# Attention with ALiBi and one key-value head: the fp32 matmuls of a step in two groups instead of three, the maxima's transpose moved

## The reference, cut to what matters

```python
q = (hidden_states @ Wq).reshape(b, s, NUM_HEADS, HEAD_DIM)
kv = hidden_states @ Wkv
k, v = (kv[..., :HEAD_DIM], kv[..., HEAD_DIM:])
scores = jnp.einsum('bqhd,bkd->bhqk', q, k) * scale
bias = slopes[:, None, None] * (pos[None, None, :] - pos[None, :, None]).astype(jnp.float32)
scores = jnp.where(causal[None, None], scores + bias[None], -jnp.inf)
attn = jax.nn.softmax(scores, axis=-1)
out = jnp.einsum('bhqk,bkd->bqhd', attn, v).reshape(b, s, h)
return out @ Wo
```

## Time and profile before

| | us |
|---|---|
| median of 3 runs | 821.62 |
| lowest and highest | 820.59, 821.73 |
| the profiled execution's own time | 822.31 |
| its span, first to last instruction | 820.5 |
| PE busy | 806.4 |
| DVE busy | 594.7 |
| POOL busy | 429.4 |
| ACT busy | 372.5 |

### The profile page before, as it was taken

The page is one execution under the profiler, slowest core; times in us unless marked ns, Lnnn a source line. Parts: engine busy times, 40 slices in busy tenths (PEclk is TensorE's granted clock), DMA queues, the critical chain, the costliest instruction groups (busy, mean ns, idle before and its releaser), DMA issues.

```text
span 820.5 us, 13647 instructions
## 1 busy us (share of the span) xinstructions
PE 806.4 (98%) x4618; PEld 583.2 (71%) x4618; DVE 594.7 (72%) x1589; ACT 372.5 (45%) x730; POOL 429.4 (52%) x313
## 2 busy tenths in 40 slices
PE   7999999999999999999999999999999999999997
PEld 5777878888665655556555555688887888888886
DVE  3877554577878889988888896255647779684877
ACT  1755536232466677676666665221401231051322
POOL 1000000000299998899889988522746298363566
PEclk9999999999999999999999999999999999999999
DMA  8867687467566655676566655462064613500012
GB/s 313 315 199 209 229 256 256 154 177 223 152 140 150 152 132 146 146 160 143 134 146 172 156 122 172 151 180 89 1 224 136 198 60 111 194 28 1 38 65 103
DMA packets 71390, 125.85 MB, mean 153 GB/s; under 512 B 7460, under 2 KB 16708, under 8 KB 71240
## 3 DMA queue, kind: packets, MB, share of 16 engines
q1 hardware_dynamic: 71312, 124.97, 52.5%
q10 hardware_dynamic: 8, 0.01, 0.0%
HBM read 85.61 MB, written 38.94 MB: 152 GB/s over the span
## 4 chain that ended last, share of the span: by engine, by line
PE 77%; DMA 7%; DVE 6%; issue 4%; ACT 4%; POOL 1%; SPq 0%; DVEq 0%; POOLq 0%; ACTq 0%
PE p_s L870 11%; PE p_st L899 9%; PE p_o L910 9%; PE p_s L978 5%; PE p_s L980 5%; PE p_s L979 5%; PE p_o L923 5%; PE p_o L809 4%; DMA inv_b<-inv_d 3%; PE p_s L809 2%; PE p_st L978 2%; PE p_st L980 2%; PE p_st L979 2%; PE p_s L1003 2%; PE p_s L1002 2%
## 5 line engine op out<-in xcount | busy, mean ns | idle before, releaser
L1452 DVE CUSTOM_DVE_ANT_0 spill<-p_s,mask 128x128 bf16<-128x128 f32 (+3 forms) x512 | 219.6, 483 | 38.3 <-PE p_s L870 37.6
L1169 ACT ACTIVATE pt<-p_st 128x512 f32<-128x512 f32 (+1 forms) x352 | 178.2, 562 | 101.1 <-PE p_st L899 100.9
L635 POOL TENSOR_SCALAR_AFFINE_SELECT pt<-pt 128x512 f32<-128x512 f32 x128 | 87.5, 696 | 238.7 <-ACT pt L1169 238.7
L870 PE MATMUL p_s<-kst,xt 98*128 98x128 f32 (+3 forms) x512 | 151.1, 343 | 0.9 <-DVE mx L1452 0.7
L899 PE MATMUL p_st<-xt,kst 100*128 100x512 f32 (+1 forms) x352 | 129.4, 387 | 0.7 <-DMA xt<-ml 0.3
L870 PEld LDWEIGHTS p_s<-kst,xt 98*128 98x128 f32 x512 | 91.4, 189 | 52.7 <-DVE mx L1452 42.7
L642 POOL TENSOR_TENSOR pt<-pt 128x1536 f32<-128x1536 f32 x32 | 111.8, 3492 | 2.7
L910 PE MATMUL p_o<-pt,vst 128*32 128x512 f32 (+3 forms) x1024 | 82.4, 439 | 0.0
L648 POOL TENSOR_TENSOR pt<-pt 128x1024 f32<-128x1024 f32 x32 | 76.7, 2396 | 0.0
L899 PEld LDWEIGHTS p_st<-xt,kst 100*128 100x128 f32 x352 | 64.5, 190 | 14.1 <-issue 5.6
L809 PE MATMUL p_o<-xt,wqh 128*128 128x512 f32 x136 | 53.1, 400 | 0.8 <-DVE xt L1603 0.8
(11 more groups left out here) (205 smaller groups left out, 1648.0 us busy)
## 6 DMA issues: line engine op xcount, KB each, us to landing
xt<-qh_d SPq DMA_DIRECT2D x64, 256.0 KB
xs<-in_x_t_dram SPq DMA_DIRECT2D x32, 256.0 KB, 6.2
qh_d<-qh SPq DMA_DIRECT2D x32, 256.0 KB, 3.2
ql_d<-ql SPq DMA_DIRECT2D x32, 256.0 KB, 4.1
xt<-ql_d SPq DMA_DIRECT2D x32, 256.0 KB
o_d<-o_st SPq DMA_DIRECT2D x32, 256.0 KB, 2.3
ob<-o_d SPq DMA_DIRECT2D x32, 256.0 KB, 5.5
xin<-in_x_dram SPq DMA_DIRECT2D x14, 512.0 KB, 7.8
```

The lines of the kernel that those rows point to most:

```text
L635: pool.affine_select(out=own, in_=own, compare_op=ALU.is_ge, fill=0.0, base=0, pattern=[[0, 4], [1, P]], channel_multiplier=-1).then_inc(c ...
L870: pe.matmul(scores_of(n), qst[s % 4][0:R_MAX, j, qb * P:(qb + 1) * P], kst[0:R_MAX, b * S:b * S + keys], start=True, stop=True).then_inc(s ...
L1169: act.activation(pt[s % 2][:, j:j + heads, PT_AT[kb]:PT_AT[kb] + KB_LEN[kb]], p_st[:, place(k) % 3, 0:heads * KB_LEN[kb]].rearrange("p (j ...
L1452: dve.tensor_tensor_reduce(spill[:, SPILL_AT[qb]:SPILL_AT[qb] + keys], scores_of(n), mask[:, S - keys:S], 1.0, LOWEST, ALU.add, ALU.max, m ...
```

## The change

Two tables that set PE's order within a step are rewritten. Nothing else differs: the same instructions run on all engines, with the same waits, and the lists of DVE, ACT, POOL and SP are the same.

```diff
-            ORDER = "xuxuxTGxuxuxuxuGuxuxxuuxGxu"
+            ORDER = "xuxuTxuxuxGuxuxuxuxuxuGxux"
 
-            GROUP = (((0,), ()), ((1, 2, 3), ()), ((), (0, 1)))
+            GROUP = (((0, 1, 2), ()), ((3,), (0, 1)))
```

## The result

The changed kernel takes 829.7 us (median of 4 runs, 828.68 to 830.46) against 821.54 for the kernel before: ratio 1.0101, 95% interval 1.0083 to 1.0118. It is slower by 8.2 us, near the forecast of 832.0. The other 1.8 us by which the medians differ lie in how executions of one kernel differ; no trace here shows where.

What follows compares the result with a forecast made beforehand. PE's order, closely coupled to DVE's maxima, was taken to set the step. Plain steps +4.5, reciprocals +4.4 and sums' copies +1.5 made +10.4 us on 822.31, so 832.7, median 832.0; range 821 to 841.

Steps and rivals of the forecast that it cites:

- The saving: PE's merged groups and the tiles behind them: 0.41 us less per step if nothing waits.
- T alone at 0.11: T by itself, outside a group, costs PE 0.11 us, as before.
- T's wait of 0.28: T needs C4's maximum from DVE, with too little work between: a wait of 0.28 us per step.
- C3's 0.22 and A4's 0.09: Behind H0, C3 waits 0.22 us for C2's maximum and A4 0.09 more for A3's.
- the loop of 1.17 us: From the end of a 512-column tile to the earliest start of a tile needing its maximum from DVE: 1.17 us.
- Steps with reciprocals, +4.4: In 12 steps DVE's reciprocals delay B2 by 0.24 us and C4's maximum and T by 0.13: +4.4 us (2.5 to 6.5).
- B2's wait of 0.24: In steps with reciprocals, B2 waits for B1's maximum, held up by a reciprocal on DVE: 0.24 us taken.
- Steps 9, 17, 25, +1.5: ACT's sums' copy delays the exponential of u1, whose bank u3 needs ahead of H0: +1.5 us (0 to 1.5).
- A shorter loop (faster): The PE-DVE loop is shorter in the new order, 0.95 us for example: -6 us, 816; chance 0.14.
- merging that saves nothing: The 0.20 us behind a group is paid at each change of kind anyway: 6.2 us on top, 838; chance 0.10.
- a longer tile behind T: Sign that T's change of kind also costs 0.20 us, so merging saves nothing: 838 us; chance 0.10.
- POOL as the wait: POOL's cut of key block 2 comes 0.5 us after H0 wants it in 30 steps: 847 us; chance 0.04.

Runs made afterwards that it cites:

- run 1: Changed kernel with H0 cut in two, key block 0 a group of its own again; 835.7 us, 1.0172 of the kernel before.
- run 2: Changed kernel with T behind C1, as in the order before, still without a group beside it; 829.5 us, ratio 1.0102.
- run 3: Changed kernel with C2 straight behind H0 and u4 and u5 behind it; 824.1 us, ratio 1.0034.
- run 5: Changed kernel with DVE's maxima of the 384- and 512-column tiles over the last 128 keys only; 818.5 us, ratio 0.9979.
- run 6: Kernel before with DVE's maxima of the 384- and 512-column tiles over the last 128 keys only; 818.7 us, ratio 0.9967.
- run 4: Changed kernel with DVE's reciprocals behind B2 and ACT's copy of the sums behind the exponential of u4; 825.5 us, ratio 1.0054.
- run 10: Changed kernel with only DVE's subtraction or multiplication for the output weights moved, from behind A3 to behind A4; 913.8 us in one run.
- run 9: Changed kernel with C2 behind H0, reciprocals behind B2, sums' copy later, B4 ahead of H1, DVE's output-weights operation behind A4 instead of A3; 907.4 us.

## Why the prediction was right, point by point

*The saving.* H0 2.07 (said 2.09), H1 1.44 (1.43), 0.31 us for a group (run 1): right. With the rule of the page "TensorE: Matmul & The Clock Gate" of the Trainium skill, section "Step-by-step: what each phase is for", a turn from one kind of matmul to the other would have cost nothing; in run 1 the tile behind the added group took 0.43 instead of 0.23, so the rows were the better guide here.

*T alone at 0.11*: right, shown by run 2, where T takes 0.11 behind a C1 that has done the waiting.

*T's wait of 0.28*: 0.26, of it 0.11 already at B1. *C3's 0.22 and A4's 0.09*: 0.22 and 0.08. Both rest on the loop of 1.17 us that was read from two small waits in the kernel before. A plain step was to be 0.15 longer and is 0.16. Over the 28 steps measured that is 4.5 us (said 4.5 for 30). That these waits are the cause is shown by runs 3, 5 and 6.

*Steps with reciprocals, +4.4*: mis-sized, and just under its own range of 2.5 to 6.5. They are 9.73, 0.20 over a plain step, so 12 x 0.20 = 2.4. B2's wait of 0.24 was 0.22 in the chain. The other part, 0.13 for a late C4 at the step's end, did not come. The term counted 0.91 us for the weights' subtraction; in the new order it takes 0.69, the next maximum starts 0.61 after it (267.04 to 267.65), and 0.61 with two reciprocals of 0.27 is 1.15, which fits into the 1.19. The prediction took the 0.91 for the operation's own price; it depends on what POOL does beside it (last section).

*Steps 9, 17, 25, +1.5*: steps 8 and 9 together took 19.55 us where 9.53 and 9.53 would be 19.06, so 0.49; three times that is 1.5. Right. That ACT's copy is the cause is shown by run 4.

*What was left out*: the kernel before had single waits of its own, three steps of 9.64 to 9.66 and one of 9.9, so 1.4 us in all, which the changed kernel doesn't show at these places. The three short ones, 0.8 us, the sum could have taken off. The long one is a matter of that one execution, a DMA of `ml` that landed late; the line of its chain:

```profile
396.03 6.67 DMA xt<-ml
```

The measured terms, 4.5 + 2.4 + 1.5 - 1.4 = 7.0, meet the 7.0 of the trace's 28 steps. So the mechanism and the size of a plain step were right. The forecast was too high, by 2.3 us against the median and by 4.0 (10.4 against 6.4) between profiled executions, through the reciprocals, the single waits and projections that were 1.0 us shorter in that execution; the errors point the same way, so it was not two of them cancelling that brought it near.

*The rivals.* A shorter loop (faster) is refuted by the rows of the four tiles; merging that saves nothing, by run 1, and a longer tile behind T, by C1's 0.24 behind it; POOL as the wait did not come: POOL releases some weight loads inside H0, but H0 kept its 2.07 us.

## What to carry to other kernels

When PE and another engine hand a few buffers back and forth, measure the loop, from the end of a tile to the earliest start of the tile that reuses its buffer (here 1.17 us), and count what PE has to do in between at each place of a new order; the saving of a merged group means nothing before that. A group of other work between two such tiles is not only cost, it hides the loop, and a long group followed by a long run of tiles makes both engines wait by turns. Small extra work on the other engine has a place where it is free and places where it isn't, and moves with the order. What an operation of DVE with both operands in SBUF takes depends on what POOL runs beside it, so its duration in the old order is no price for the new one.

## What the runs showed of the hardware that was not expected

DVE's subtraction of two SBUF operands beside POOL's addition of two SBUF operands took 3.34 us (median of 16) instead of 0.69. The page "GPSIMD Engine Reference" of the Trainium skill (section "1. Specifications") says that POOL shares its SBUF interfaces with DVE and that they contend when a DVE instruction has two SBUF inputs; the runs agree. They also show that the one that started later stood still. In run 10 DVE started 0.68 us after POOL and lost 3.34 - 0.69 = 2.65 of the 2.79 us that POOL's addition still had to run. In two steps of run 9 DVE started 0.06 or 0.07 us ahead of POOL; it took its own 0.69 us, and POOL's addition 3.99 or 4.00 instead of 3.47. The first of the two:

```profile
328.01 0.69 DVE L1469 TENSOR_TENSOR wol<-ob,woh 128x512 fp32r<-128x512 f32 x1
328.08 3.99 POOL L642 TENSOR_TENSOR pt<-pt 128x1536 f32<-128x1536 f32 x1
```

This is also why the subtraction was shorter in the changed order than in the kernel before. Before, in step 13, it started at 342.04, while POOL's cut ran to 342.48, and it ended 0.54 us after the cut; in the changed order it starts before the cut (or with it, in steps with reciprocals), and it is the cut that takes 0.93 us instead of 0.63. First the cut of the kernel before, then the changed kernel:

```profile
341.85 0.63 POOL L635 TENSOR_SCALAR_AFFINE_SELECT pt<-pt 128x512 f32<-128x512 f32 x1
...
267.04 0.69 DVE L1469 TENSOR_TENSOR wol<-ob,woh 128x512 fp32r<-128x512 f32 x1
267.29 0.93 POOL L635 TENSOR_SCALAR_AFFINE_SELECT pt<-pt 128x512 f32<-128x512 f32 x1 [0.88 <-ACT pt L1169]
```

DVE's maxima, with one operand in PSUM, took their usual 0.69 us beside the same addition (at 270.35 in the changed kernel, POOL's addition from 268.31 to 271.80).

PE's clock fell in runs 9 and 10. In run 9 PE waited 2.25 us for DVE, ran on for 2.09 us at a granted clock of 0.97, and then came this H0 (a line of the windows: stretch, then us of PE, PEld, DVE, ACT and POOL with their instructions, granted clock, DMA share and GB/s):

```profile
268.85:272.56 3.71, 3.71 (x25) 0.99 (x25) 1.33 (x9) 0.44 (x1) 1.40 (x2) 0.56 0.37 112
```

The granted clock in it was 0.56, near the lower level of 1.2 GHz, and H0 took 3.71 us instead of 2.07. Not every such wait was followed by this: in run 10 PE waited 1.92 us ahead of the step from 268.65 to 280.25, and the granted clock in that step was 1.00; in the next step it was 0.87, and H0 took 2.88. What decides it these runs don't show. So runs 9 and 10 lost time twice: in the wait, and in the matmuls behind it.
